# A two-layer max graph convolution with an expert layer: tiles in steps of three ranks, joined maxima, rows split by VectorE, a ScalarE normalisation

## What is computed

```python
def _graph_conv_max(x, src, dst, W_rel, b, W_root):
    agg = jax.ops.segment_max(x[src], dst, num_segments=N)
    agg = jnp.where(jnp.isfinite(agg), agg, 0.0)
    return agg @ W_rel.T + b + x @ W_root.T
...
def reference(x, src, dst, ...):
    h = _layernorm(x)
    h = relu(_graph_conv_max(h, src, dst, W1_rel, b1, W1_root))
    h = relu(_graph_conv_max(h, src, dst, W2_rel, b2, W2_root))
    x = x + h
    z = _layernorm(x)
    probs = softmax(z @ Wr, axis=0)             # over the 1250 tokens
    vals, idx = top_k(probs.T, 512)             # 512 tokens for each of 8 experts
    h = gelu(einsum('ecd,edf->ecf', z[idx], W1) + b1)
    out_e = einsum('ecf,efd->ecd', h, W2) + b2
    return x + scatter_add(vals[..., None] * out_e, idx)
```

## Time and profile before

| | us |
|---|---|
| median of three runs | 1026.27 (1025.17 to 1026.45) |
| the profiled execution | 1024.63 |
| its span | 1022.6 |
| PE busy, share | 716.0, 70% |
| DVE busy, share | 719.3, 70% |
| POOL busy, share | 572.0, 56% |
| ACT busy, share | 236.2, 23% |
| mean granted TensorE clock | 0.886 of 2.4 GHz |

### The profile page before, as it was taken

How to read it: one execution, slowest core, us unless ns; L and a number is a source line. 1 busy time by engine, 2 the same in 40 slices (tenths; PEclk the granted TensorE clock), 3 DMA queues, 4 the chain that set the end, 5 groups by cost and what they waited for, 6 DMA issues and landing times.

```text
span 1022.6 us, 9802 instructions
## 1 busy us (share of the span) xinstructions
PE 716.0 (70%) x2593; PEld 322.9 (32%) x2593; DVE 719.3 (70%) x1313; ACT 236.2 (23%) x281; POOL 572.0 (56%) x561
## 2 busy tenths in 40 slices
PE   0329248999998889345887878776874512999997
PEld 0224013333333333112333333332331311444442
DVE  3769838888999988514899999989998596331110
ACT  0275231233333333002012222112200100122222
POOL 5650476566777777765445555666566203445533
PEclk9759669999999999657999999988987755999999
DMA  5740576566666766679556666666664702556746
GB/s 136 221 116 2 165 208 200 162 182 187 192 202 191 206 190 212 215 252 245 148 177 200 178 186 192 204 207 186 183 196 151 276 0 76 93 120 104 131 55 81
DMA packets 66460, 169.54 MB, mean 166 GB/s; under 512 B 16633, under 2 KB 21029, under 8 KB 66400
## 3 DMA queue, kind: packets, MB, share of 16 engines
q0 software_dynamic: 42240, 130.79, 47.0%
q1 hardware_dynamic: 16887, 18.45, 6.4%
q10 hardware_dynamic: 7288, 19.76, 5.7%
HBM read 145.72 MB, written 23.11 MB: 165 GB/s over the span
## 4 chain that ended last, share of the span: by engine, by line
DVE 31%; PE 30%; issue 16%; DMA 10%; POOL 7%; DVEq 2%; ACT 2%; POOLq 0%; SPq 0%; ACTq 0%
PE pp L1097 8%; PE pp L1417 6%; DVE weights L906 6%; PE pp L1404 5%; DVE acc L895 5%; DMA mem<-tab,ic 5%; POOL mem L838 4%; PE prow L1068 3%; DMA weights<-hotd 2%; PE prow L1037 2%; PE prow L1056 2%; DVE acc L975 2%; DVE mem L1274 2%; DVE mem L608 1%; DVE weights L908 1%
## 5 line engine op out<-in xcount | busy, mean ns | idle before, releaser
L838 POOL DMA_INDIRECT mem<-tab,ic x372 | 391.9, 1054 | 230.3 <-issue 100.3
L1097 PE MATMUL pp<-weights,slots 128*128 128x512 bf16 x1200 | 303.9, 403 | 136.2 <-DVE acc L895 85.0
L895 DVE TENSOR_TENSOR acc<-acc,pp 128x1024 f32<-128x1024 f32 x180 | 219.0, 1217 | 31.8 <-PE pp L1097 25.5
L906 DVE TENSOR_TENSOR weights<-weights,mem 128x1024 f32<-128x1024 f32 x166 | 203.3, 1225 | 25.3 <-SPq L805 14.2
L1097 PEld LDWEIGHTS pp<-weights,slots 128*128 128x128 bf16 x1200 | 117.2, 102 | 321.2 <-DVE acc L895 100.1
L1068 PE MATMUL prow<-weights,aggT 128*128 128x512 f32 x160 | 84.1, 654 | 13.7 <-ACT aggT L1162 13.7
L1385 DVE COPY weights<-prow 128x512 f32<-128x512 f32 x32 | 20.8, 687 | 98.7 <-PE prow L1037 98.1
L1456 POOL DMA_INDIRECT out<-mem,node_of x32 | 50.3, 1571 | 67.6 <-ACT mem L1434 58.8
L1056 PE MATMUL prow<-weights,rootT 128*128 128x512 f32 x160 | 74.2, 606 | 0.0
L1417 PE MATMUL pp<-weights,mem 128*128 128x512 f32 x128 | 63.5, 618 | 0.0
L908 DVE SCALAR_TENSOR_TENSOR weights<-carry,cap,mem 128x1024 f32<-128x1024 f32 x20 | 25.7, 1284 | 48.7 <-SPq L805 39.7
(11 more groups left out here) (361 smaller groups left out, 792.0 us busy)
## 6 DMA issues: line engine op xcount, KB each, us to landing
slots<-ttd ACTq DMA_DIRECT2D x20, 640.0 KB, 5.7
mem<-tab,ic POOLq DMA_INDIRECT x372, 3.8
weights<-in_L_ffn_W SPq DMA_DIRECT2D x9, 512.0 KB, 9.6
weights<-in_L_ffn_W ACTq DMA_DIRECT2D x7, 512.0 KB, 4.1
xnd<-xin ACTq DMA_DIRECT2D x10, 256.0 KB, 3.2
mem<-in_x SPq DMA_DIRECT2D x2, 1120.0 KB
tab<-mem SPq DMA_DIRECT2D x1, 2240.0 KB
weights<-in_L_gnn_W_rel SPq DMA_DIRECT2D x2, 1024.0 KB, 12.4
```

The costliest lines, as they stand in the source:

```text
L838: g.indirect_dma_start(ring[:, h * PAIR + k, :], None, tables[l], bass.IndirectOffsetOnAxis(ic[:, j * PAIR + k:j * PAIR + k + 1], 0))\
L895: v.tensor_tensor(acc[:, :, :], acc[:, :, :], pp[j % 2][:, :, :], ALU.max).then_inc(S["pa"], 1)
L906: v.tensor_tensor(accg, accg, pair, ALU.max).then_inc(S["done"], 1)
L1097: ins = t.matmul(pp[j % 2][:, i, :], sel[u][:, j * KP + i, :], hot[:, j, w, :], start=w == 0, stop=w == 2)
```

## The change

1. **Tiles in steps of three ranks.** `recs` is loaded by three strided DMAs instead of one: tiles 1 to 3 take the rank groups 2, 5 and 8 (counted from 0 behind tile 0's), tiles 4 to 6 take 1, 4 and 7, tiles 7 to 9 take 0, 3 and 6. The heaviest group, which shares nodes with tile 0, is tile 3 (`HEAVY`). The ring pairs of the ten tiles are then 6, 8, 10, 14, 8, 9, 11, 7, 9 and 11.
2. **First pairs joined.** `acc` begins as the maximum of the tile's first ring pair and the first picked pair, `accg` as the maximum of the second and the third ring pair (`first_three`). In the heavy tile `accg` still begins from the carry. Tile 0 handles its ten picked pairs first and its ring pairs after them.
3. **Plain rows split when layer 2 begins.** In layer 1 nothing is clamped or split, and `hotd` is gone. At the start of layer 2 SyncE loads plain float32 rows of `tab2` into `stage` in six groups; in tile 10 VectorE computes the high and the lowest part of each of the ten blocks (`high`, `lowest`) and ScalarE the middle one (`middles`), and each pair of matmuls waits for its block. TensorE does tile 10's transposes and product with W_root ahead.
4. **ScalarE normalises.** In layer 2 VectorE makes the guess only (`guess`); the Newton steps and `xin` are ScalarE's (`refine`) for all tiles but the last. `L989` goes: the test is folded into the instruction behind it.
5. **The head's gathers.** The gathers of own rows and of `x` move ahead of the last list work on GpSimd, and the write of `tab1` now waits for the edge lists to land.

The diff, cut to its core:

```diff
-HPARTS = ((0, 2), (2, 5), (5, NC))
-HSTARTS = {lo: i for i, (lo, hi) in enumerate(HPARTS)}
+HPARTS = ((0, 1), (1, 2), (2, 4), (4, 6), (6, 8), (8, NC))
+HGROUP = [i for i, (lo, hi) in enumerate(HPARTS) for _ in range(lo, hi)]
+HEAVY = 3
...
-        s.dma_start(recs[:, 1:NQ, :], recd[LIGHT:N, :].rearrange("(q p) c -> p q c", p=P)).then_inc(S["recs"], 16)
+        ranked = recd[LIGHT:N, :].rearrange("(q p) c -> p q c", p=P)
+        for i, first in enumerate((2, 1, 0)):
+            s.dma_start(recs[:, 1 + 3 * i:4 + 3 * i, :], ranked[:, first:NQ - 1:3, :]).then_inc(S["recs"], 16)
...
+        for q in range(NQ):
+            s.wait_ge(s_run[q], 16)
...
+        after(g, cv, n_nodei)
+        input_rows(range(HQ, NQ))
+        g.wait_ge(S["tab"], n_tab)
+        first_rows(range(HQ, NQ))
+        after(g, ca, n_low[NC - 1])
+        first_rows(range(0, HQ))
+        input_rows(range(0, HQ))
...
-                        s.dma_start(hot[lo:hi, c0:c1, :, :].rearrange("p c w d -> p c (w d)"), hotc[lo:hi, c0:c1, :])\
-                            .then_inc(s_hx[i], 16)
+                        s.dma_start(stage[lo:hi, c0:c1, :], tabc[lo:hi, c0:c1, :]).then_inc(s_hx[i], 16)
...
+            def first_three(k, lo):
+
+                v.wait_ge(S["ready"], first_pair + lo + (FLYING + 1))
+                v.wait_ge(S["pairs"], k * PAIRS + 1)
+                v.tensor_tensor(acc[:, :, :], in_ring(lo), pp[0][:, :, :], ALU.max).then_inc(S["pa"], 1)
+                v.wait_ge(S["pa"], k * PAIRS + 1)
+                v.sem_inc(S["apart_v"], 1)
+                if k % NQ == HEAVY:
+                    v.wait_ge(S["ready"], first_pair + lo + (FLYING + 2))
+                    v.wait_ge(S["done"], first_pair + lo + SUBS)
+                    v.scalar_tensor_tensor(accg, carry[:, :].unsqueeze(1).to_broadcast([P, 2, D]), cap[:, :],
+                                           in_ring(lo + 1), ALU.min, ALU.max).then_inc(S["done"], 2)
+                    pool_pair(lo + 2)
                 else:
-                    v.scalar_tensor_tensor(accg, carry[:, :].unsqueeze(1).to_broadcast([P, 2, D]), first, pair,
-                                           ALU.min, ALU.max).then_inc(S["done"], 1)
-
-            def clamp(q):
-
-                v.wait_ge(S["h"], q + 1)
-                if q:
-                    v.wait_ge(S["hl"], q)
-                v.tensor_scalar(hst[:, :], own_row[q], TOP, None, ALU.min).then_inc(S["hc"], 1)
+                    v.wait_ge(S["ready"], first_pair + lo + (FLYING + 3))
+                    v.wait_ge(S["done"], first_pair + lo + SUBS)
+                    v.tensor_tensor(accg, in_ring(lo + 1), in_ring(lo + 2), ALU.max).then_inc(S["done"], 3)
...
+            def high(c):
+
+                v.wait_ge(s_hx[HGROUP[c]], 32)
+                v.tensor_scalar(hot[0:CN, c, 0, :], stage[0:CN, c, :], TOP, None, ALU.min).then_inc(S["hh"], 1)
+                v.wait_ge(S["hh"], c + 1)
+                v.scalar_tensor_tensor(stage[0:CN, c, :], stage[0:CN, c, :], TOP, hot[0:CN, c, 0, :], ALU.min, ALU.subtract)\
+                    .then_inc(S["hr"], 1)
+
+            def lowest(c):
+
+                v.wait_ge(S["hm"], c + 1)
+                v.tensor_tensor(hot[0:CN, c, 2, :], stage[0:CN, c, :], hot[0:CN, c, 1, :], ALU.subtract).then_inc(S["hl"], 1)
...
+                elif k == NQ:
+                    high(0)
+                    high(1)
+                    lowest(0)
+                    high(2)
+                    lowest(1)
+                    first_three(k, lo)
+                    pe_pair(k, 1)
+                    for j in range(2, PAIRS):
+                        if j + 1 < NC:
+                            high(j + 1)
+                        lowest(j)
+                        if j == 5:
+                            with v.Fori(3, m) as i:
+                                pool_pair(lo + i)
+                        if j == 8:
+                            pool_pair(lo + m)
+                        pe_pair(k, j)
+                    pool_pair(lo + m + 1)
+                else:
+                    first_three(k, lo)
+                    pe_pair(k, 1)
...
-                    if k == NQ and j in HSTARTS:
-                        t.wait_ge(s_hx[HSTARTS[j]], 32)
+                    if k == NQ:
+                        t.wait_ge(S["hl"], j + 1)
...
+            def refine(q):
+
+                a.wait_ge(S["rc"], 4 * q + 4)
+                n = 3 * NEWTON * q + 2 * q
+                for i in range(NEWTON):
+                    a.activation(rvb[:, :], rs2[:, :], ACT.Square).then_inc(S["ra"], 1)
+                    a.wait_ge(S["ra"], n + 3 * i + 1)
+                    a.activation(rvb[:, :], rvb[:, :], ACT.Identity, bias=half3[:, :], scale=rva[:, :]).then_inc(S["ra"], 1)
+                    a.wait_ge(S["ra"], n + 3 * i + 2)
+                    a.activation(rs2[:, :], rs2[:, :], ACT.Copy, scale=rvb[:, :]).then_inc(S["ra"], 1)
+                    a.wait_ge(S["ra"], n + 3 * i + 3)
+                n += 3 * NEWTON
+                a.activation(nm2[:, :], mv2[:, 0:1], ACT.Copy, scale=rs2[:, :]).then_inc(S["ra"], 1)
+                a.wait_ge(S["ra"], n + 1)
+                a.activation(nm2[:, :], nm2[:, :], ACT.Copy, scale=-1.0).then_inc(S["ra"], 1)
+                a.wait_ge(S["ra"], n + 2)
+                if q:
+                    a.wait_ge(S["nT"], q)
+                    a.wait_ge(S["xns"], 16 * q)
+                a.activation(xin[:, :], xs[q], ACT.Identity, bias=nm2[:, :], scale=rs2[:, :]).then_inc(S["xn"], 1)
 
```

219 lines of the change are left out of this document (107 added, 112 removed).

## The result

The changed kernel takes 991.9 us (median of 4 runs, 990.4 to 992.5) where the kernel before takes 1026.2 on the same chip (1025.2 to 1026.5): ratio 0.9665, 95% interval 0.9649 to 0.9682. The forecast was 984 with a range of 964 to 1001, so sign and range hold. The saving is 34 us where 42 were forecast, and behind that sum stand misses of both signs. The profiled execution has a span of 989.9 us against 1022.6.

A forecast was written before the change was run, and what follows sets the result against it. It took VectorE to bound layer 2, TensorE the front and VectorE the back of layer 1 tiles, DMAs between the layers. Terms -14 - 5 + 8 - 31 = -42 took 1024.6 to 982.6, median 1.6 higher: 984 us, range 964 to 1001.

The forecast's parts named there:

- The likeliest case: Whole kernel: the regular forecast, three stages gaining and the step between the layers losing, 984 us; chance 0.58.
- cheap blocks: Rival, tile 10: clock stays high and the ring lands early, so the step gains 2 us, 974 us; chance 0.20.
- late gathers: Rival, all tiles: VectorE waits for ring pairs, 1 us in each of 19 tiles, 1003 us; chance 0.13.
- busy time counts: Rival, whole kernel: VectorE's saved busy time counts in full, -66 with the head, 960 us; chance 0.07.
- slower: Rival, layer 2: ScalarE's chain of 11 dependent instructions ends a tile, slower than before above 0.85 us each; chance 0.02.
- Head and tile 0: Start to tile 0's `fin`: earlier lists and gathers, picked pairs first, -14 us, bounds -16 to -10.
- the cover is thick: Head: delaying the `tab1` write some 10 us costs nothing, since its row gathers have until about 116 us.
- Layer 1: Tiles 1 to 9: dropped splits and the heavy tile's new place gain, low clock costs, -5 us, bounds -12 to +4.
- the front is TensorE's: Layer 1 tiles up to picked pair 5: TensorE sets the time, so VectorE's two saved maxima gain nothing.
- the term against it: Layer 1 tiles of ten or more ring pairs: TensorE at low clock after longer gaps, 1 us in four tiles.
- The step: Tile 9's `fin` to tile 10's: VectorE waits for matmuls in each splitting block, +8 us, bounds -2 to +16.
- Layer 2: Tiles 11 to 19: VectorE's front and back shorten, 3.5 us per tile, -31 us, bounds -36 to -22.

The follow-up runs named there:

- e1: Changed kernel with tile 10's maximum over each picked pair moved behind the next block's `lowest`; 1061.6 us on chip A, ratio 0.9727 to the kernel before.
- e2: Changed kernel with ten of the head's twenty row gathers held back until both selector loads landed; 1090.6 us on chip A, ratio 1.001 to the kernel before.
- e5b: Changed kernel with the edits of e1 and e2, and tile 10's second-and-third ring pair maximum moved behind the third `lowest`; 967.3 us on chip C, ratio 0.944.
- e8: Kernel of e5b with all twenty row gathers back behind the list work's last product; 969.6 us on chip C, ratio 0.9439 to the kernel before.
- e4b: Changed kernel with layer 1's first pairs taken one by one again in tiles 1, 2 and 4 to 9; 1068.2 us on chip B, ratio 0.9874.
- e7: Kernel of e5b with tiles in rank order again, the heaviest last, and the records in one DMA; 969.7 us on chip C, ratio 0.9459.
- e3: Changed kernel with layer 2's normalisation steps and `xin` back on VectorE; 1088.2 us on chip A, ratio 0.9954 to the kernel before.
- e3b: Same kernel as e3, run beside the changed kernel on chip B; 1076.9 us, ratio 0.9908 to the kernel before.
- e6: Kernel of e5b with the second-and-third ring pair maximum behind picked pair 1, in all tiles but each layer's first; 966.8 us on chip C, ratio 0.9454.

## Why the prediction was right, and where its steps were not

**The likeliest case happened.** The three stages that were to gain did, the one that was to lose did, and the rivals "cheap blocks", "late gathers", "busy time counts" and "slower" did not. On chips A and B less is gained (1.6% on B), behind waits that the traces do not name. That the total came within 8 us is in part luck, since layer 1 made up for 4.3 us of the misses. "Cheap blocks" was a matter of order and not of the clock: e1 built it.

**Head and tile 0: forecast -14, measured -8.7.** The direction was right; two sizes and one edit costed at nothing were off. The edge lists are there 3.1 us earlier (68.38 against 71.48) where I took 4, TensorE turns the counts at 103.69, a little later than before (102.96), and of the 2.1 us at the list work's end 1.4 are left. I wrote that the row gathers of `tab1` have until 116 us, "so the cover is thick". That was asked only of the gathers. The step that failed is that their new place, from 104.76 us on, puts them in front of the `ttd` write (110.82) on the DMA engines. It costs 3.2 us up to the first picked pairs (13.5 us from the write to them before, 16.7 after; e2, e5b: 13.6 and 13.2). These come at 127.51 instead of my 123.7. The ring gathers start 2.9 us earlier than before (134.59 against 137.44) and not 6. The remaining 1.4 us are gaps and a wait of 0.77 for the last ring pair in tile 0. e8 gives the worth of a place without the collision: 1.6 us in tile 0, and nothing that the totals show, since the tile takes its ring pairs last.

**Layer 1: forecast -5, measured -9.3.** The part on which most hung held: the front is TensorE's (e4b), tiles of nine ring pairs take 26.5 and 26.9 us before and 26.5 after, with VectorE idle 1.60 us ahead of picked pair 3 where before it had its ring maxima to do. Here tile 5:

```profile
282.50 2.75 PE L1165 MATMUL pp<-weights,slots 128*128 128x512 bf16 x12
283.99 2.55 DVE L899 TENSOR_TENSOR acc<-acc,pp 128x1024 f32<-128x1024 f32 x2 [1.60 <-PE pp L1165]
```

The tile of 14 went from 41.9 to 36.4 (forecast 36.5), and with the old order the two tiles of eight take 25.2 instead of 26.5 (e7; forecast 1.2 each). In the new order they take 27.1, as the first tile behind tile 0, and 26.2, behind the heaviest. The tile of seven went from 27.6 to 25.2, the 2.4 of the forecast, but that is luck: my sum had 26.3 and 23.9, and in the old order without the splits (e7) it takes 28.4, so its gain is the place's and not the splits'. What failed is the term against it: I charged 4 us for TensorE at the low clock behind longer gaps, in the tiles of ten and eleven. Those take 27.9, 29.7 and 29.5 us, against 28.0, 29.4 and 30.7 before. No such cost is there, and without that term the sum was -8.5, beside -9.3 measured. The order was worth 7.0 us in this layer (e7) and not 3.7.

**The step: forecast +8, measured +14.9.** The mechanism is the one described, and a plain block cost 5.8 us where I took 5.5 (bounds 4.4 and 5.8): TensorE's groups took 2.72 us, the low level, in all blocks but the two with a ring maximum, which as forecast cost nothing. The blocks as a whole took 43.8 us (447.4 to 491.2), forecast 43. Three other sizes were off. The first `high` starts at T+16.75 instead of T+14, since product (5.7 us), scatter (1.76) and its landing put the index DMAs at T+12.4 and not at T+9.2. The first picked maxima are over at T+33.9 instead of T+30, just past the end of the range that I had given (33.5): third ring pair at T+31.6. And the 2 us that I took off because first waits might overlap did not come. My bounds for this term ended at +16. What plain rows bring to layer 1 does not pay for this: with the old order and no splits it takes 260.8 us (e7), 3.3 less than before. By these two stages the third edit as built lost some 11 to 12 us (an estimate, since it was not undone by itself), and with the order of e5b it gains about as much.

**Layer 2: forecast -31, measured -28.6.** Sorted by ring pairs the tiles gained 3.4 us (7 pairs), 3.3 and 2.5 (8), 2.2 and 3.8 (9), 4.1 (10), 3.6 and 3.5 (11), 2.3 (14); forecast was 3.5 each. With the old order layer 2 takes 266.9 us (e7), 31.5 less than before: the edits in the tiles were sized right in the sum (single tiles gain 2.2 to 4.1), and the 3 us that are missing are the price of the new order, on which I had set nothing in this layer. How the 31.5 divide between the two edits in these tiles is not shown: undoing ScalarE's part cost 1.9 us in a tile of nine on chips A and B (e3, e3b), where the forecast has 2.55 for its back. ScalarE's eleven small instructions take 0.20, 0.39 and 0.30 us by their operands, 3.5 us with hand-over from 634.98 to 638.48, and `xin` 0.81: 4.3 us, in the middle of the 3.4 to 5.4 given, and hidden. I had leaned to the lower end, "the same form", and the rows say that the form with two pointer operands costs twice the plain one.

The Trainium skill, "ScalarE: Activation LUTs", Rules for kernel authors, budgets about 0.3 us per activation; the trace agrees in the mean (3.5 us / 11 = 0.32). Its advice to keep multiplies and adds on VectorE is not borne out here, though VectorE does this work faster (2.55 us in e3 with the guess, against 4.3 without it): e3 and e3b put it there, and a tile of nine ring pairs grows by 1.9 us, since VectorE is the bound and ScalarE has the time.

**The sum.** The misses (+5.3, -4.3, +6.9, +2.4, -1.0) add to 9.3 us in the profiled execution; the median lies 7.9 above the forecast. Two sums of the prediction are off without touching it: VectorE's front in layer 2 loses 2.4 us and not 2.3, and the last rival at 1.5 us for each small instruction comes to 1090 us by its own terms and not 1075.

## What to carry to other kernels

When one engine makes the input of another and takes its result back, look at the order on the first: the consumer's result must not be taken right behind the release that starts it. One step of its own work in between took 18 to 19 us out of the step between the layers (e1) and needed no instruction more. Where the two totals lie inside each other's scatter, as on chip C from e6 on, compare stages, and know first how far a stage moves between kernels that share its code. When a transfer is moved forward, ask not only whether its data and its slot are free in time but whose short transfer, on which a chain waits, it will then stand beside. And a term "against", put in for caution without a row that shows it (the clock cost in layer 1, the overlap in the step), is as likely to be wrong as one put in from hope.
